# A recurrent stage on one Trainium2 core: one gate product per token tile instead of one per head, and a new order of the 31 steps

## The reference, cut to what matters

```python
def step(S, xs):                                  # the recurrence over chunks of a sequence
    qi, ki, ui, wi = xs
    attn = jnp.where(tri_lo, qi @ jnp.swapaxes(ki, -1, -2), 0.0)
    u_i = ui - wi @ S
    o = qi @ S + attn @ u_i
    return (S + jnp.swapaxes(ki, -1, -2) @ u_i, o)
...
stats = jnp.concatenate([_stats(local_short), _stats(local_long), _stats(delta_out), _stats(vh)], -1)
hs_exp = jnp.broadcast_to(hs[:, :, None, :], (b, l, H, hs.shape[-1]))
gate_in = jnp.concatenate([hs_exp, stats], -1)    # 256 token features + 16 statistics, per head
hgate = jax.nn.gelu(gate_in @ mlp_w1 + mlp_b1, approximate=False)
logits = hgate @ mlp_w2 + mlp_b2
probs = jax.nn.softmax(logits / temp, -1)
```

## Time and profile before

| | us |
|---|---|
| median of 3 runs | 6020.67 (6015.63 to 6024.58) |
| profiled execution, device time | 6031.09 |
| its span, first to last instruction | 6029.3 |
| PE matmul busy | 5421.1 (90%) |
| PE weight load busy, beside the matmuls | 4326.3 (72%) |
| DVE busy | 4262.5 (71%) |
| ACT busy | 2668.0 (44%) |
| POOL busy | 2549.7 (42%) |

### The profile page before, as it was taken

The page is one execution under the profiler, slowest core; times in us unless marked ns, Lnnn a source line. Parts: engine busy times, 40 slices in busy tenths (PEclk is TensorE's granted clock), DMA queues, the critical chain, the costliest instruction groups (busy, mean ns, idle before and its releaser), DMA issues. The chain is left out here.

```text
span 6029.3 us, 119845 instructions
## 1 busy us (share of the span) xinstructions
PE 5421.1 (90%) x42776; PEld 4326.3 (72%) x42776; DVE 4262.5 (71%) x13841; ACT 2668.0 (44%) x6214; POOL 2549.7 (42%) x3716
## 2 busy tenths in 40 slices
PE   6999999999999999979966645999999999999987
PEld 5888888888888888859954433777777777777765
DVE  4777777777777777752127885888887888888861
ACT  2555555555555555531133321444444444444441
POOL 1222222222222222210057751666666666666660
PEclk9999999999999999989965555999999999999998
DMA  1011101101110110118855542222222222222211
GB/s 41 29 34 36 33 31 36 36 29 34 36 36 29 34 36 29 34 39 186 201 140 147 141 111 63 61 62 61 61 61 61 61 61 62 61 62 61 61 35 44
DMA packets 603925, 373.22 MB, mean 62 GB/s; under 512 B 336528, under 2 KB 589264, under 8 KB 603344
## 3 DMA queue, kind: packets, MB, share of 16 engines
q1 hardware_dynamic: 532880, 329.91, 19.9%
q10 hardware_dynamic: 65664, 16.78, 1.2%
q0 software_dynamic: 4800, 18.88, 1.0%
HBM read 212.59 MB, written 137.10 MB: 58 GB/s over the span
## 5 line engine op out<-in xcount | busy, mean ns | idle before, releaser
L526 POOL TENSOR_TENSOR a_shift<-a_mean_var,a_eps 128x2 f32<-128x2 f32 x256 | 71.3, 278 | 1833.5 <-DVE a_mean_var L736 1833.5
L2125 PE MATMUL c_bank<-c_xT,c_gate 128*128 128x512 f32 x1024 | 499.8, 611 | 1.9 <-ACT c_statsT L1878 1.9
L750 DVE SCALAR_TENSOR_TENSOR a_cv<-a_raw,a_taps,a_cv 128x256 f32<-128x256 f32 x1152 | 461.9, 479 | 19.5 <-ACT a_cv L628 10.0
L820 PE MATMUL a_bank<-a_w,a_hidden 128*128 128x256 f32 x2048 | 459.1, 382 | 0.9 <-ACT a_hidden L613 0.9
L918 PE MATMUL a_bank<-a_turned,a_w 128*128 128x256 f32 x2048 | 453.0, 379 | 1.1 <-ACT a_turned L574 1.1
L820 PEld LDWEIGHTS a_bank<-a_w,a_hidden 128*128 128x128 f32 x2048 | 383.8, 190 | 71.8 <-issue 20.6
L918 PEld LDWEIGHTS a_bank<-a_turned,a_w 128*128 128x128 f32 x2048 | 384.0, 190 | 51.2 <-ACT a_turned L574 1.6
L1775 POOL TENSOR_TENSOR c_expd<-c_e,c_logit 128x16 f32<-128x16 f32 x128 | 371.7, 2904 | 51.1 <-DVE c_logit L1961 38.7
L1761 POOL TENSOR_TENSOR c_stats<-c_l2sq,half 128x16 f32<-128x16 f32 x128 | 373.4, 2917 | 17.8 <-DVE c_l2sq L1950 17.8
L2129 PEld LDWEIGHTS c_bank<-c_statsT,c_gate_stats 128*128 128x128 f32 x2048 | 270.1, 192 | 123.8 <-issue 123.8
L1345 POOL TENSOR_TENSOR i_coef<-i_base,i_exponent 128x12 f32<-128x12 f32 x128 | 298.6, 2332 | 76.7 <-issue 53.5
(11 more groups left out here) (294 smaller groups left out, 14194.1 us busy)
## 6 DMA issues: line engine op xcount, KB each, us to landing
a_x<-in_x SPq DMA_DIRECT2D x64, 256.0 KB, 3.3
scratch_xb<-a_xb SPq DMA_DIRECT2D x64, 256.0 KB, 2.1
scratch_q<-a_qkv_rows SPq DMA_DIRECT2D x64, 256.0 KB, 2.2
scratch_k<-a_qkv_rows SPq DMA_DIRECT2D x64, 256.0 KB, 2.7
scratch_v<-a_qkv_rows SPq DMA_DIRECT2D x64, 256.0 KB, 3.0
b_window<-scratch_v SPq DMA_DIRECT2D x8, 2048.0 KB, 22.2
scratch_long<-b_out ACTq DMA_DIRECT2D x8, 2048.0 KB, 24.6
scratch_short<-b_out POOLq DMA_DIRECT2D x8, 2048.0 KB, 18.4
```

The source lines that it names most:

```text
L750: ins = dve.scalar_tensor_tensor(cv[s][:, n, c], raw[s][:, n, c, j:j + TOK], taps[:, n, c, j:j + 1], cv[s][:, n, c], ALU.mult, ALU.add)
L820: ins = pe.matmul(dst[:, t * D:(t + 1) * D], src[s][:, c, tile_cols(t)], weight[:, c], start=(c == 0), stop=(c == chunks - 1))
L2125: pe.matmul(dst[:].rearrange("p (h t) -> p h t", h=H), gate1[:, c, cols], xT[sl][:, c:c + 1].broadcast_to([P, H, P]), start=(c == 0), stop ...
```

## The change

The token part of the gate is computed once per tile, in a step of its own (`base`): two matmuls of 128x256 with the tokens as rows. ACT copies it to SBUF. In `pre`, the token part of each head's 128 columns then comes from a transpose of this copy against the identity (four transposes of 128x128 for each half, instead of the two 512-column matmuls), which opens the bank; the statistics part is added as before. The list has 31 steps with new numbers, and `DEPTH` goes from 6.969 to 5.999, so that a tile's steps are spread over six tiles' time instead of seven.

```diff
-    DEPTH = 6.969
+    DEPTH = 5.999
...
-    shares = [("load", 0.01), ("keys", 5.22), ("load_src", 0.01), ("turn_x", 2.02), ("turn_qk", 2.2), ("gram", 1.78),
...
+    shares = [("load", 3.98), ("keys", 0.01), ("load_src", 3.39), ("turn_x", 0.06), ("turn_qk", 1.04),
...
+        base = slots("base", [P, D], 2)
...
+            def gate_base(i, s):
+                done_with(act.activation(base[s % SLOTS][:], full(act, i, s, "base")[:, 0:D], ACT.Copy), s, "base")
...
+            def gate_base(i, s):
+                dst = open_bank(i, s, "base", "xT")
+                for c in range(C):
+                    ins = pe.matmul(dst[:, 0:D], xT[s % SLOTS][:, c], gate1[:, c], start=(c == 0), stop=(c == C - 1))
+                fill(ins, s, "base")
...
             def gate(i, s):
+
                 sl = s % SLOTS
                 for m in range(C):
                     cols = slice(m * P, (m + 1) * P)
-                    dst = open_bank(i, s, f"pre{m}", "statsT")
-                    for c in range(C):
-                        pe.matmul(dst[:].rearrange("p (h t) -> p h t", h=H), gate1[:, c, cols],
-                                  xT[sl][:, c:c + 1].broadcast_to([P, H, P]), start=(c == 0), stop=False,
-                                  skip_group_check=True)
+                    dst = open_bank(i, s, f"pre{m}", *(("statsT", "base") if m == 0 else ()))
+                    for h in range(H):
+                        pe.matmul(dst[:, h * P:(h + 1) * P], base[sl][:, cols], ident[:], start=(h == 0), stop=False,
+                                  is_transpose=True, skip_group_check=True)
                     for h in range(H):
                         ins = pe.matmul(dst[:, h * P:(h + 1) * P], gate1_stats[:, h, cols], statsT[sl][:, :],
                                         start=False, stop=True, skip_group_check=True)
```

More of the change, by code:

```diff
@@ L1502, in phase_c @@
     LOADS = 5 * 16
-    shares = [("load", 0.01), ("keys", 5.22), ("load_src", 0.01), ("turn_x", 2.02), ("turn_qk", 2.2), ("gram", 1.78),
[L1506 to L1509, removed]
+    shares = [("load", 3.98), ("keys", 0.01), ("load_src", 3.39), ("turn_x", 0.06), ("turn_qk", 1.04),
+              ("gram", 0.01), ("kS", 1.34), ("solve0", 2.44), ("carry1", 2.51), ("solve1", 2.15), ("carry2", 2.36),
+              ("solve2", 0.48), ("carry3", 1.7), ("solve3", 2.28), ("o", 0.89), ("dS", 0.27), ("stats", 9.01),
+              ("l2", 1.58), ("base", 0.44), ("statsT", 2.01), ("pre", 1.5), ("logits", 4), ("softmax", 2.63),
+              ("mix", 2.24), ("rms", 1.54), ("oT", 3.32), ("Wo", 1.42), ("lnC_stats", 1.86), ("lnC", 0.01),
+              ("lnD_stats", 3.45), ("lnD", 0.07)]
     run = partial(run_pipelined, written=WRITTEN)
@@ L1512, in phase_c @@
     jobs_of = {"turn_x": ["xT"], "turn_qk": ["qkT"], "gram": ["G0", "G1"], "kS": ["kS"], "o": ["o"], "dS": ["dS"],
-               "statsT": ["statsT"], "pre": ["pre0", "pre1"], "logits": ["logitsT", "logits"], "oT": ["oT"], "Wo": ["Wo"]}
+               "statsT": ["statsT"], "base": ["base"], "pre": ["pre0", "pre1"], "logits": ["logitsT", "logits"], "oT": ["oT"], "Wo": ["Wo"]}
     for b in range(BLOCKS):
@@ L1879, in _ @@
                                                                 ACT.Copy), s, "statsT"),
+                "base": gate_base,
                 "pre": hidden, "logits": logits_sbuf, "mix": mix_short, "rms": square_o, "oT": turned_o,
@@ L2158, in _ @@
             stages = {"turn_x": turn_x, "turn_qk": turn_qk, "gram": gram, "kS": k_state, "o": o_of, "dS": new_state,
-                      "statsT": turn_stats, "pre": gate, "logits": logits, "oT": turn_o, "Wo": project}
+                      "statsT": turn_stats, "base": gate_base, "pre": gate, "logits": logits, "oT": turn_o, "Wo": project}
             for b in range(BLOCKS):
```

## The result

The changed kernel took **6052.6 us** in the median (6031.3 to 6069.3, 11 runs), the kernel before 6023.6 on the same chip (6015.6 to 6028.6): a ratio of 1.0048, 95% interval 1.0037 to 1.006. It is slower by half a per cent; 5964 was forecast, and the range ended at 6035. The profiled execution has a span of 6054.3 us.

A forecast was written before the change was run, and what follows sets the result against it. Three near-equal loops were taken to bound the kernel, not PE's load. Loop D at 16.2 us plus 0.3 for the clock, less an overlap, gave 16.35 against 16.77; with the ends, 5964 us, range about 5880 to 6035.

The forecast's parts named there:

- The loops: Per-tile chains of waits through gate, DVE and solve, each fitting into the 16.57 us beat, within 0.2 us of each other.
- D: Loop from DVE's state update through logits, POOL's exponent and softmax: 16.4 us before, binding at 16.2 after the change.
- The lock: POOL's wide multiplications hold DVE's two-SBUF-input operations by shared ports; the new order frees 0.6 us a tile.
- The load: Transfers behind the store of y reach POOL's keys about 0.2 us late; `mix` locks DVE 0.3, plus 0.1 us.
- The clock: PE's clock falls to 1.2 GHz in small work before Wo, about 4 tiles of 10, adding 0.3 us a tile.
- The ends: Filling and draining with six tiles in flight instead of seven: 4 us shorter, bounds 0 and 15.
- The sum: 127 tiles at 16.35 instead of 16.77 us save 53 us, with the ends 57, giving 5964 us.
- Rival 5: Slower, as the clock falls in nearly every tile before Wo: +38 us, 6033 to 6090 us, chance 0.12.
- The doubt about transposes: By the Trainium skill, transposes don't count as busy for the clock; the gate's eight would be weak, giving Rival 5's time.

The follow-up runs named there:

- e1: The new gate alone, in the order and depth of the kernel before, with `base` as a step of its own: 6379.6 us, 1.0591 of before.
- e12: e1 plus unused 128x256 matmuls, two at the head of each gate half and one in the gap of logits: 6003.5 us, 0.9972 of before.
- e2: The new order and depth alone, with the old gate of 512-column matmuls and no `base`: 6223.8 us, 1.0335 of before.
- e9: The changed kernel plus one unused 128x256 matmul in kS's bank ahead of kS and one in the gap of logits: 5943.2 us, 0.987 of before.
- e11: The changed kernel with the edits of e9 and e10 together: 5893.0 us, 0.9787 of before.
- e10: The changed kernel with SP's five load transfers moved ahead of the stores of y and xc: 6040.7 us, 1.0031 of before.
- e6: The changed kernel plus four unused 128x128 transposes ahead of solve2 and four in the gap of logits: 5984.4 us, 0.9933 of before.
- e5: The changed kernel plus one unused 128x256 matmul ahead of solve2 and one in the gap of logits: 5973.9 us, 0.9914 of before.
- e4: The changed kernel plus one unused 128x256 matmul ahead of solve0 and one ahead of solve3: 6139.4 us, 1.0179 of before.

## Why the prediction was wrong, step by step

- **The loops: right.** "Three loops within 0.2 us of each other", D binding, PE's relief not on it. Shown by e1, whose quiet tile gained 0.1 us from 1.8 us less work, and by the quiet tile of after (0.17 us of waiting for the exponent). The gate's 1.8 us: 5.41 − 2.75 − 0.97 = 1.7. PE's waits are 1.17 us, where 1.5 were forecast, the longest at solve2 and not at solve0 or solve3.
- **The lock: right**, and its size too: 652 to 178 ns at L1946. It goes with the order, not with the gate: it is there in e12 and in the quiet tiles of e1, and in e2, with the new order and the old gate, the two operations have medians of 189 and 179 ns. The 0.3 us that I charged for `mix` lying elsewhere on DVE is not there in a tile whose load is on time: L1950 takes 0.17 us. That, and the 0.1 of the load, is most of why the quiet beat with the load on time is 15.6 to 15.7 and not 16.2.
- **The load: right in kind, too small in size.** I had it 0.2 us late, with the keys 1.4 us behind the update; they start 1.8 us behind it in the median, and POOL waits 62.9 us over 112 tiles, 0.56 each. (The "15 us to spare" before is the whole lead of the first transfer over the keys, of which 4.0 are needed: 11 to spare. Nothing rests on it.) I charged 0.3 us a tile for it (0.2 of lock, 0.1 of its own); e9 against e11 prices it at 50 us, 0.4 a tile, where hardly any falls are left, and after against e10 at 12 us where they stay.
- **The clock: the step that failed.** "So I expect the fall in about 4 tiles of 10 ... 0.7 to 0.8 us each, 0.3 a tile on the mean (0.1 to 1.1)." Measured: 71 of 127 tiles have some of a fall, and the mean is 17.00 − 15.65 = 1.35 us above the undisturbed tile. That still holds the late load; e10, without it, has 16.78 − 15.65 = 1.13 us a tile, 143 us in all, with 62 falls: 2.3 us each. The place was right (the stretch from `kS` to Wo). The count was somewhat too low (4 tiles in 10 against 5 to 6), the price by a factor of three, and the price was wrong in three ways. I took a fall for 3.4 us, as the one row showed; 26 of the 66 now last twice that. I let only Wo, o and dS be late, by 1.7 us; from the last solves on it is 6.50 − 3.65 = 2.85. And I gave PE 0.5 us of slack and credited a lock escaped, though most of the lock was already out of my own sum, and the slack was 0.3: dS was done at 4134.88 for an update at 4135.31, of which a disturbed tile still keeps 0.1 (4321.27 and 4321.38). The rows at hand would have given the price: 16.77 − 16.57 = 0.2 us a tile with a fall in 1 tile of 10 is 2 us a fall. With that and the 4 in 10 of the forecast, the term is 0.8 us instead of 0.3, and 16.2 + 0.8 is slower than before. (That it also lands on the measured 17.00 is luck: 16.2 was 0.5 too high and 4 in 10 too low.)
- **The ends: right.** The first update is 2.0 us earlier and the rest behind the last 1.6 us shorter; forecast 4.
- **The sum.** From first to last update it is (5868.4 − 3709.6) − (5841.8 − 3711.6) = +28.6 us; less 3.6, that is the 25 us between the two spans. With no falls and the load on time, 127 × (15.65 − 16.77) = −142 us and the same ends would give 5878 on the median of before; e11, whose beat is 15.71, measured 5893.

Rival 5 is what happened, in time (6033 to 6090) and in cause, with a chance of 0.12. Its own condition, "from about 8 tiles in 10", was too strict by the same error: e10, with 62 falls in 127 tiles and the load on time, has a mean beat of 16.78, that of before, so falls in about half the tiles use up the whole gain, and after had some of a fall in 56%. The doubt about transposes stood on the wrong leg, since by e6 they do count here. That the falls go, and the time with them, once PE has work in place of its waits, is shown by e12 against e1 and e9 against after. What the small blocks do is not as clear: as filler they left 31 falls where a full matmul left 4, at the same time of the kernel. What exactly the chip weighs stays open.

## What to carry to other kernels

When PE is the busiest engine but doesn't set the beat, removing its work creates waits, and what the waits do to the clock can cost more than the work did: look at PEclk first, find the stretches of PE between two large matmuls, and count the waits and small blocks in them. Price a fall by the mean beat against the undisturbed one, over all the falls of the trace, and not by working out one example. A dummy matmul in a bank that is already free, at a place where PE waits anyway, is a cheap probe of this and here a cure; the same one on the chain that others wait for lengthened the undisturbed tile (by 0.36 us in e5, 0.64 in e4, load included). In an in-order queue, ask of each entry what it waits for: a transfer moved past one waiting store gained a tile, not the time of the store.

## What was not expected of the hardware

- Once down, the clock can stay down for long in a kernel that goes on working: 23.9 us in e1, 17 to 20 in seven falls of e4, while in before nearly every fall lasted 3.4. At half speed PE waited no less at solve2 in e1 (2.11 us cold, 1.84 quiet), and the clock came back after half a tile to one and a half.
- Transposes as filler held the clock up nearly as well as full matmuls (11 and 4 falls, 66 without), and 32x32 blocks about half as well (31).
- The two wide multiplications of POOL held DVE's operations with two SBUF inputs (654 ns in e12, 178 in after); the powers of 2.9 us, under which DVE's L1975 and L1976 start, held nothing.
- One store that waits for its data holds back every transfer behind it on its queue: by e10, the five transfers of a load start 19.4 us ahead of their use instead of 3.9 once they stand ahead of it.
